# First layer of a graph network: reorder by transfers, or by products on turned x

## The reference, cut to what matters

```
weight = jnp.einsum('rb,bio->rio', w_comp, bases)        # 32 x 8, 8 x 256 x 256
xw = jnp.einsum('ni,rio->nro', h, weight)                # 6250 x 32 x 256
msg = xw[src, rel_type] * norm
out = jax.ops.segment_sum(msg, dst, num_segments=h.shape[0])
...
x = _layernorm(x + relu(out))
```

## Time and profile before

| what | us |
|---|---|
| median of 3 runs | 7217.41 |
| lowest and highest run | 7214.42, 7223.92 |
| span of the profiled execution | 6364.3 |
| set-up | 0 to 77.2 |
| table of layer 0 | 77.2 to 805.3 |
| first walk, table of layer 1 | 805.3 to about 1900 |
| the rest | about 1900 to 6364.3 |

### The profile page before, as it was taken

How to read it: one execution, slowest core, us unless ns; L and a number is a source line. 1 busy time by engine, 2 the same in 40 slices (tenths; PEclk the granted TensorE clock), 3 DMA queues, 4 the chain that set the end, 5 groups by cost and what they waited for, 6 DMA issues and landing times.

```text
span 6364.3 us, 77713 instructions
## 1 busy us (share of the span) xinstructions
PE 4985.1 (78%) x19175; PEld 3374.5 (53%) x19176; DVE 3946.2 (62%) x9442; ACT 1596.1 (25%) x3091; POOL 3597.4 (57%) x3549
## 2 busy tenths in 40 slices
PE   5999869999987777776666666279999997776766
PEld 3555547777773433333444444257787874333333
DVE  5555566666646666666666666876666665655555
ACT  3555534444440000001222222123333331000000
POOL 0000067777757777776777777223333335777776
PEclk8888889999997777777888887679999997667676
DMA  6999956666654444445777777267666774344343
GB/s 231 364 361 365 371 190 216 217 216 217 216 198 122 124 124 124 124 124 154 242 244 244 242 245 245 76 197 237 236 233 234 238 241 139 116 117 116 116 117 111
DMA packets 476381, 1279.57 MB, mean 201 GB/s; under 512 B 137938, under 2 KB 262716, under 8 KB 412533
## 3 DMA queue, kind: packets, MB, share of 16 engines
q1 hardware_dynamic: 315557, 832.27, 37.5%
q0 software_dynamic: 160464, 443.17, 24.2%
HBM read 636.68 MB, written 587.04 MB: 192 GB/s over the span
## 4 chain that ended last, share of the span: by engine, by line
PE 58%; DVE 11%; issue 10%; DMA 9%; POOL 6%; SPq 3%; ACT 1%; DVEq 1%; POOLq 0%; ACTq 0%
PE ps L1409 27%; PE ps L1584 11%; PE ps L1433 8%; PE ps L1567 5%; DMA table<-A 5%; POOL ring L630 3%; POOL A L630 2%; PE ps L1369 2%; DMA work<-place_dram 2%; DVE W L816 2%; DVE A L816 2%; PE ps L1384 1%; SPq L476 1%; SPq L355 1%; DMA A<-gat_table,ix 1%
## 5 line engine op out<-in xcount | busy, mean ns | idle before, releaser
L618 POOL DMA_INDIRECT ring<-table,idx x2490 | 2366.4, 950 | 1640.0 <-DVEq L840 774.8
L1409 PE MATMUL ps<-ring,W 128*128 128x256 f32 x3320 | 1189.5, 476 | 440.4 <-DVE W L816 278.0
L1409 PEld LDWEIGHTS ps<-ring,W 128*128 128x128 f32 x3320 | 683.3, 229 | 869.2 <-DVE W L816 399.6
L816 DVE TENSOR_SCALAR W<-iota,dloc,norm 128x128 f32<-128x128 f32 x1660 | 597.6, 361 | 766.7 <-PE ps L1409 756.8
L1409 PE MATMUL ps<-ring,A 128*128 128x256 f32 x1660 | 724.6, 543 | 271.5 <-DVE A L816 210.8
L643 POOL TENSOR_TENSOR ring<-ring,work 128x1024 f32<-128x1024 f32 x208 | 405.7, 1951 | 809.8 <-DMA ring<-rows_dram 809.8
L1584 PE MATMUL ps<-W_r,work_r 128*128 128x512 f32 x1960 | 701.1, 440 | 0.0
L834 DVE TENSOR_TENSOR X<-X,ps 128x256 f32 x1660 | 688.2, 415 | 17.2 <-PE ps L1409 15.2
L1409 PEld LDWEIGHTS ps<-ring,A 128*128 128x128 f32 x1660 | 340.2, 248 | 620.2 <-DVE A L816 367.6
L1433 PE MATMUL ps<-W_r,work_r 128*128 128x512 f32 x1568 | 560.0, 439 | 0.0
L1148 DVE TENSOR_TENSOR X<-X,ps 128x264 f32 x830 | 352.4, 425 | 329.4 <-PE ps L1567 272.8
(11 more groups left out here) (239 smaller groups left out, 7045.1 us busy)
## 6 DMA issues: line engine op xcount, KB each, us to landing
table<-A SPq DMA_DIRECT2D x294, 1024.0 KB, 6.2
ring<-rows_dram SPq DMA_DIRECT2D x208, 528.0 KB, 4.6
table<-A SPq DMA_DIRECT2D x49, 1280.0 KB, 5.4
table<-W SPq DMA_DIRECT2D x49, 1280.0 KB, 6.9
rows_dram<-ring SPq DMA_DIRECT2D x52, 1056.0 KB, 4.8
rows_dram<-A SPq DMA_DIRECT2D x52, 1056.0 KB, 4.6
ring<-table,idx POOLq DMA_INDIRECT x2490, 2.8
A<-W SPq DMA_DIRECT2D x264, 128.0 KB, 5.3
```

The source lines that it names most:

```text
L618: pool.indirect_dma_start(out=f_ring[:, s % NR, :], out_offset=None, in_=src, in_offset=bass.IndirectOffsetOnAxis(ap=idx[:, s:s + 1], axis ...
L816: return dve.tensor_scalar(marks_[:, k % G, :], iota[:, :], dloc[:, k:k + 1], norm[:, k:k + 1], ALU.is_equal, ALU.mult).then_inc(wk.onehot ...
L1409: pe.matmul(ps[:, s % banks, 0:D], marks_[:, s % G, :], f_ring[:, s % NR, :], start=True, stop=True).then_inc(wk.step_done, 1)
```

## The change

The 8 bases no longer come to lie side by side by transfers. They do so because the products are computed turned: the bases are the stationary operand, with columns picked so that one PSUM bank holds, for two windows, 128 partitions = 2 strips x 8 bases x 8 outputs. A constant matrix `comb` (64 partitions by 32 relations x 8 outputs) then combines the bases for 8 outputs at a time, in two strips of 64 partitions, with nodes on partitions in the result.

- The unit is a pair of windows (`NSB` = 25; the last has one window), in `OQ` = 8 steps. A step m gives 32 of the 256 outputs. `base_products(m)` is 12 matmuls of 256 columns, `combine(m, w)` 12 of 256 columns for each window w, into two banks, which ScalarE and VectorE copy, one each.
- ScalarE makes the high part and VectorE the low part straight from the PSUM bank (`high_xb`, `low_xb`); `l_xb` and `l_S` are gone.
- Four table buffers: two halves of the outputs (t) by two windows (w). `store_half(k, t, w)` writes 128 of 256 outputs for each relation and node, 2 MB in pieces of 512 bytes. A table row is now in the plain order of nodes, and the index is node x 32 + relation.
- x is no longer loaded whole in set-up, but for each pair (`load_x`), two pairs ahead; `turn_x(k)` turns it.

Besides, the constant matrix is made by one multiplication on VectorE, and six index operations of set-up are gone. The core of the diff:

```diff
-                load(X[:, 0:NW1, :], x[0:NW1 * P].rearrange("(w p) c -> p w c", p=P))
...
-                def reorder_bank(k, n):
-                    sp.wait_ge(l_xb_free, XBANKS * k + n + 1)
-                    for b in (2 * n, 2 * n + 1):
-                        sp.dma_start(l_S[k % 3][b:P:BASES, :].rearrange("i (g o) -> i g o", o=D),
-                                     l_xb[:, b * D:(b + 1) * D]).then_inc(l_s_in[n], 16)
...
+                rows = table.rearrange("(w p) (r t o) -> w t p r o", p=P, r=R0, t=2)
+                x_rows = x.rearrange("(k w p) c -> k p w c", p=P, w=2)
+
+                def load_x(k):
+                    if k >= 2:
+                        sp.wait_ge(l_turned, k - 1)
+                    sp.dma_start(l_x[k % 2], x_rows[k]).then_inc(l_x_in[k % 2], 16)
+
+                def store_half(k, t, w):
+                    m = OQ * k + (t + 1) * OQ // 2 - 1
+                    sp.wait_ge(l_act, banks_before(m, w) + 1)
+                    sp.wait_ge(l_dve, banks_before(m, w) + 1)
+                    sp.dma_start(rows[2 * k + w, t], l_table[2 * t + w]).then_inc(l_t_free[2 * t + w], 16)
+
+                load_x(0)
+                load_x(1)
+                for k in range(NSB):
+                    for t in range(2):
+                        for w in range(blocks_of(k)):
+                            store_half(k, t, w)
+                    if k + 2 < NSB:
+                        load_x(k + 2)
...
-                ch(dve.tensor_copy(src_i, srcf[:, :]))
-                ch(dve.tensor_scalar(block_i, src_i, P - 1, None, ALU.bitwise_and))
...
+                ch(dve.scalar_tensor_tensor(idx[:, 0:KP], srcf[:, :], float(R0), types[:, walk0.tcol, :], ALU.mult, ALU.add))
...
+                def low_xb(m):
+                    dve.wait_ge(xb_high, m + 1)
+                    dve.tensor_tensor(l_low[m % 2], ps[:, 1 + m % 2, :].rearrange("p (h n) -> p h n", h=2), l_high[m % 2].bitcast(F32),
+                                      ALU.subtract).then_inc(xb_low, 1)
+
+                def to_table(m, w):
+                    k, q = m // OQ, m % OQ
+                    if q % (OQ // 2) == 0 and k >= 1:
+                        dve.wait_ge(l_t_free[2 * (q // (OQ // 2)) + w], 16 * k)
+                    dve.wait_ge(l_full, 2 * banks_before(m, w) + 2)
+                    dve.tensor_copy(table_place(m, w, 1), comb_bank(w, 1).rearrange("p (h r o) -> p h r o", h=2, o=OS)).then_inc(l_dve, 1)
...
+                def turn_x(k):
+                    pe.wait_ge(l_x_in[k % 2], 16 * (k // 2 + 1))
                     if k >= 1:
-                        pe.wait_ge(l_xt_ready, k)
+                        pe.wait_ge(x_low, k)
...
+                def combine(m, w):
+                    if w == 0:
+                        pe.wait_ge(xb_low, m + 1)
+                    if m >= 1:
+                        pe.wait_ge(l_act, banks_before(m - 1, w) + 1)
+                        pe.wait_ge(l_dve, banks_before(m - 1, w) + 1)
+                    terms = [(l_high, comb_high), (l_low, comb_high), (l_high, comb_low)]
+                    for h in range(2):
+                        for n, (rows, c) in enumerate(terms):
+                            for s in range(2):
+                                part_ = slice(s * 64, (s + 1) * 64)
+                                ins = pe.matmul(comb_bank(w, s)[:, h * CC:(h + 1) * CC], rows[m % 2][part_, h, w * P:(w + 1) * P], c[part_, :],
+                                                start=(n == 0), stop=(n == 2))
...
+                for m in range(OQ * NSB):
+                    k, q = m // OQ, m % OQ
+                    if m + 1 < OQ * NSB:
+                        base_products(m + 1)
+                    for w in range(blocks_of(k)):
+                        combine(m, w)
+                    if q == OQ // 2 - 1 and k + 1 < NSB:
+                        turn_x(k + 1)
```

More of the change, by code:

```diff
@@ L126, in build @@
[L126 to L131, removed]
@@ new lines, in build @@
+        l_x = [flat_ring[:, 2560 + u * 512:2560 + (u + 1) * 512].rearrange("p (w c) -> p w c", w=2) for u in range(2)]
+        comb_raw = targets1[:, 0:CC]
+        comb_row = targets1[:, CC:CC + R0]
+        comb_place = targets1[:, CC + R0:CC + R0 + OS]
+        l_xt_high, l_xt_low = ([work_r[:, (2 * v + u) * 512:(2 * v + u + 1) * 512].rearrange("p (c n) -> p c n", c=2) for u in range(2)] for v in range(2))
+        assert BASES * 2 * OS == P and 3 * half <= 2 * NSC and 4 * BW + half <= 2 * NSC and 2560 + 1024 <= U * GROW and 2 * CC == 512
@@ L243, in build, with blocks_of, banks_before @@
         z_zero, z_ps = sem("z_zero"), sem("z_ps")
[L246 to L249, removed]
+        (b_split_high, b_split_low, c_made, c_high, c_low, l_turned, x_high, x_low, l_xb_full, xb_high, xb_low, l_full, l_act,
+         l_dve) = (sem("l_" + n) for n in ("b_high", "b_low", "c_made", "c_high", "c_low", "turned", "xt_high", "xt_low", "xb_full", "xb_high",
+                                           "xb_low", "full", "act", "dve"))
+        l_x_in = [sem(f"l_x_in{u}") for u in range(2)]
         l_t_free = [sem(f"l_t_free{h}") for h in range(4)]
+        def blocks_of(k):
+            return min(2, NW1 - 2 * k)
+        def banks_before(m, w):
+            k = m // OQ
+            return OQ * sum(blocks_of(i) for i in range(k)) + (m % OQ) * blocks_of(k) + w
         class Walk:
@@ L343, in layer0_transfers @@
             def layer0_transfers(_):
[L344 to L350, removed]
@@ L1208, in deviation @@
+                high_x(0)
+                act.wait_ge(b_split_low, 8)
+                high_xb(0)
+                for m in range(OQ * NSB):
+                    k, q = m // OQ, m % OQ
+                    if m + 1 < OQ * NSB:
+                        high_xb(m + 1)
+                    for w in range(blocks_of(k)):
+                        to_table(m, w)
+                    if q == OQ // 2 and k + 1 < NSB:
+                        high_x(k + 1)
             def deviation(g):
@@ L1359, in turn_window, with base_products @@
                     ins.then_inc(l_turned, 1)
[L1361 to L1364 removed]
+                def base_products(m):
+                    k, q = m // OQ, m % OQ
+                    if q == 0:
+                        pe.wait_ge(x_low, k + 1)
                     if m >= 2:
[L1366 to L1371 removed]
@@ L1388, in layer0_products @@
[L1388 to L1402 removed]
+                        pe.wait_ge(xb_low, m - 1)
@@ new lines, in base_products @@
+                    terms = [(b_high, l_xt_high, c) for c in range(2)] + [(b_low, l_xt_high, c) for c in range(2)] + [(b_high, l_xt_low, c) for c in range(2)]
+                    for h in range(2):
+                        for n, (w, rows, c) in enumerate(terms):
+                            ins = pe.matmul(ps[:, 1 + m % 2, h * 2 * P:(h + 1) * 2 * P], w[:, c, q, h, :], rows[k % 2][:, c, :],
+                                            start=(n == 0), stop=(n == len(terms) - 1))
+                    ins.then_inc(l_xb_full, 1)
```

228 lines of the change are left out of this document (83 added, 145 removed).

## The result

The changed kernel takes **7347.25 us**, median of 4 runs (7341.6 to 7356.85), against 7218.94 (7214.42 to 7223.92) for the kernel before beside it: a ratio of 1.0177, 95% interval 1.0163 to 1.0192, or +128 us. The forecast was 7285 (7200 to 7405), slower: the sign and the range held, the size was 60 us short.

What follows compares the result with a forecast made beforehand. Transfers were taken to bound the kernel, TensorE next. First pair, 22 more loops (842.5) and last stores (30.7) end the stage at 873 against 805: 7217.4 + 68 = 7285 us, range 7200 to 7405.

Steps and rivals of the forecast that it cites:

- Part 1: Table-stage transfers: 512-byte pieces at 28.2 ns, 7.2 us a store; a window 14.8 us of DMA against 14.86.
- The 77 ns of the earlier trace: Packet price at the program's last store, 1 KB pieces, 30 ns above the line; set aside as a special shape.
- Part 2: TensorE in the table stage: a step costs 3.1 us, two windows 25.3 us at the full clock.
- Part 3: Set-up without the whole load of x: gain 3 us; first store issued at 99 against 105.3.
- the edge records: Set-up: without the 6.4 MB of x ahead, they land about 3 us sooner than 38.6.
- Part 4: Table stage: TensorE waits for x queued behind stores; loop 29.7 us a pair, 31.7 with clock loss.
- 16.8 and 12.9 + 2: Loop per pair: 16.8 us from store issue until x lands, 12.9 to the next issue, 2 for lost clock.
- the case that I gave 0.52: The forecast's main case in the table stage: loops of 30 to 34 us, 7240 to 7345; chance 0.52.
- Transfers alone: Table stage: the wait for x is hidden, all stores run end to end; +20 us, 7238; chance 0.12.
- Faster at line rate: Table stores: 512 bytes move at the rate of 8 KB; -63 us, 7154; chance 0.10.
- packets dearer: Table stores: 8.9 us each, +187, 7404, chance 0.10; or 14.9 us each, +775, 7992, chance 0.03.
- TensorE the bound: Table stage: strips run one after the other or weights aren't hidden; step 4.5 us, +235, 7450; chance 0.07.

Runs made afterwards that it cites:

- whole-row version: Changed kernel with the second window combined four steps later, three whole-row buffers, 16 KB store runs and x loaded early: 6304.71 us, ratio 0.9911 to kernel before.
- second run: The changed kernel, unaltered, measured again on another chip beside the kernel before: 6484.87 us against 6362.15, ratio 1.0198.

## Why the prediction was right, and where it was short

**What bounds the kernel, right, but one assumption false.** Transfers with TensorE next. I took 853 us to lie around the span and to be unchanged. They are not there: the profiled execution of the changed kernel takes 7356.85 us with a span of 7355.1, and on the chips of the experiments the kernel before takes 6361 to 6362 us as a whole, which fits the span of 6364.3. The trace of before and its runs are not of one speed. That it did no harm was luck: the table stage happens to be equal in all of them, and nothing that the forecast used showed it.

**Part 1, the transfers, right.** The stage's queue while only stores run, 412 to 417 us:

```profile
DMA packets 2838, 1.45 MB, mean 290 GB/s; under 512 B 2, under 2 KB 2838, under 8 KB 2838
```

16 x 5 us / 2838 = 28.2 ns a packet, the number forecast, so 7.2 us a store. Where nothing else held the transfers the stage ended at 836.8, 826 forecast: 3 us are the later start, the rest is 1% on the price. The 77 ns of the earlier trace rows was rightly set aside; what makes that store dear no run shows. The price is one of long streams and not of every moment: right behind the load of x the 512-byte packets came faster, 24.6 ns each from 406.11 to 409.7 us, and why is open:

```profile
DMA packets 2339, 1.20 MB, mean 334 GB/s; under 512 B 0, under 2 KB 2339, under 8 KB 2339
```

A window's transfers were forecast at 14.8 us against 14.86 before. The first holds: with x early, 87 stores from 150 to 800 us make 14.9. The second is 14.4 in mid-stage, since 14.86 had the start of the stage in it. So transfers alone were no even trade but some 0.5 us a window dearer. The forecast didn't use that comparison, it added up times of the changed kernel. The Trainium skill, DMA: Bandwidth & Descriptors, Specifications, gives 512 bytes as the size from which a transfer moves at line rate. The stores show 290 GB/s against the 421 of the earlier trace rows, so it doesn't hold here; by it the stage would have ended near 742. With 16 KB pieces in the changed kernel's own order it ended at 778.6, and only with x early as well at 747.8, so even at the full rate the change would have gained some 27 us and not the 63 of that rival.

**Part 2, TensorE, close.** Half a step starts every 1.62 us (412.06 to 413.68 above), a step takes 3.24 where 3.1 was forecast. A pair with its four transposes is some 26.3 for 25.3. The copies never bound it.

**Part 3, set-up.** The stage starts at 75.7 for 77.2: 1.5 us gained, 3 forecast. The term that failed is the edge records: VectorE's first use of them starts at 37.81 for 38.61, 0.8 us sooner and not 3, and another 0.7 is gained in the copies behind it. The first store was issued at 102.07, 99 forecast; before, 105.33.

**Part 4, right in mechanism, the failed term.** The loop through the x load is real (95 us went when x moved ahead), and it has the order and place forecast. Its two halves were sized 16.8 and 12.9 + 2; they measured 17.95 and 16.20:

- *From the store's issue to x turned, +1.1.* With the data at the forecast 15.15, what lies around them is 2.8 us, not 1.6. I had taken the 1.6 from one lone store. Some 0.4 of it is a gap between the stores' data and x's, near 404.4, in which the 16 engines are idle (busy tenths, 400.8 to 405.8 in 40 slices):

```profile
DMA  9999999999999999999999999990127999999999
```

- *From x turned to the next issue, +1.3.* The clock's loss was nearly right: 2 us forecast, and against the full-clock rows, (2.91 - 1.69) + (2.41 - 1.69) make 1.9, and the turn, 1.12 where one ahead of the loop took 0.66 (row of 101.52 below), makes it 2.4. The busy table of that stretch shows which level it is, half speed, 1.2 GHz, after 5.45 us idle, then back to 2.4; the second fence is the turn ahead of the loop:

```profile
406.11:409.70 3.59, 3.58 (x16) 3.38 (x16) 0.00 (x0) 0.00 (x0) 0.00 (x0) 0.50 1.12 334
409.70:412.06 2.36, 2.36 (x25) 2.21 (x25) 1.24 (x2) 1.19 (x2) 0.00 (x0) 0.65 1.02 278
412.06:422.30 10.24, 10.24 (x114) 9.44 (x113) 6.64 (x12) 6.29 (x12) 0.00 (x0) 1.00 0.72 201
```

```profile
101.52 0.66 PE L1365 MATMUL ps<-ident,ring 128*128 128x128 f32 x4
```

  The rest are steps of 3.24 for 3.1 (0.5 over three and a half) and 0.4 in copies and semaphores.

Added up: the first loop starts 3.4 us late (115.4 for 112), 23 turns take 784.9 us where I had 730.5 (the first 33.1, then 31.7 each), and the last stores 31.2 for 30.7. That is 58 of the 60 us. An error of 2.4 us in a loop is small beside 31.7, but a loop has no slack and is paid 23 times. At 34.1 us and 7347 the result lies just past the upper edge of the case that I gave 0.52 (30 to 34 us, 7240 to 7345), by its mechanism; the wider range held it.

**The rivals.** "Transfers alone" is excluded for the changed kernel by its DMA share of 0.89 and came true once the order was changed. "Faster at line rate" and "packets dearer" are excluded by 28.2 ns. "TensorE the bound" is excluded with its step of 4.5 us, since a step takes 3.24; at 3.24 TensorE is what holds the whole-row version. The marks named beforehand came as DMA share 0.89 for 0.91, 249 GB/s for 265, 23 waits of 5.6 us for x instead of 3 to 5, and 1 us of waits for table stores.

## What to carry to other kernels

A transfer that the engines wait for must be issued ahead of the bulk stores that it doesn't depend on: placed behind two of them on one queue it cost 95 us here, and nothing else about it had to change. Before a change trades one kind of transfer for another, price both by packets and bytes together: 28.2 ns for 512 bytes, 311 for 8 KB. And when the result of a new layout comes in short pieces, look for an order of work that completes rows in SBUF before they are stored: no version with 512-byte pieces beat the kernel before, and with x early in both, whole rows brought the first gather forward by 87 us. A short wait of TensorE can cost more than its length: here one of 5.5 us was followed by 2.3 us lost to half clock, one of 1.3 us by none.

## What was not expected of the hardware

**Issuing short pieces holds SyncE.** The second of two stores of 4096 pieces holds SyncE for 5.4 us and the load behind it for 8.2 (rows of 422.95 and 428.39 above), where 1 MB in 8 KB pieces takes 0.37. The first of the two, of the same form but issued when the queues were empty, holds it for 0.54 (rows of 388.17 and 422.32). So it isn't the count of pieces alone: in these rows the long issues come behind pieces that still wait. In the whole-row kernel, with 16 KB pieces:

```profile
308.65 0.81 SPq L373 DMA_DIRECT2D table<-A  x2
309.51 0.90 SPq L367 DMA_DIRECT2D X<-in_x  x1
```

In the changed kernel it cost little, since the loads stood behind those stores in any case. The load's issue ended at 403.07, some 1 us before the stores' data did, and the gap of 0.4 us near 404.4 may be its price; no run separates that. An engine with other work to do should not issue such transfers.

**One program, two speeds, 13% apart.** The changed kernel's profiled span is 7355.1 us in the first comparison and 6481.8 on the chip of its second run. All of the difference lies behind the table stage. A stretch of the first walk in the slower execution, then in the other:

```profile
1100.00:1500.00 400.00, 340.63 (x1458) 269.50 (x1456) 200.30 (x645) 149.62 (x316) 254.94 (x269) 0.96 0.55 183
```

```profile
1100.00:1500.00 400.00, 377.20 (x1729) 306.48 (x1728) 243.66 (x772) 183.70 (x376) 302.74 (x320) 1.00 0.65 215
```

In 400 us POOL issues 269 gathers in one and 320 in the other. One gather's instruction takes the same 0.95 us in both; what grows is the idle time before it (group of L622 in each page, the slower first):

```profile
L622 POOL DMA_INDIRECT ring<-table,idx x2490 | 2368.6, 951 | 2262.1 <-DVEq L843 901.1
```

```profile
L622 POOL DMA_INDIRECT ring<-table,idx x2490 | 2366.1, 950 | 1763.6 <-DVEq L843 901.8
```

Why is open; that it is the chip is inferred, since no chip shows both speeds here. For this change it means that the +1.8% and +2.0% of the two comparisons are the same 123 to 128 us.
